# A macaron layer on one core: two fp32 tiles first, another preparation table, layers finished at their last sum, a router in four steps

## The reference

```
x = x + 0.5 * ffn(norm(x));  x = x + attention(norm(x));  x = x + 0.5 * ffn(norm(x))
attention: 16 heads of 64, causal softmax(q k^T / 8) v, then W_out
ffn: gate = u Wg^T + bias; the 4 largest of 8 are chosen, weights = softmax over them
     out = swiglu(u; Ws) + sum over 8 experts of weight_e * swiglu(u; W_e)
     swiglu(u) = (sigmoid(h) * h * v) W3^T, h = u W1^T, v = u W2^T, 341 hidden units each
```

## Time and profile before

| | |
|---|---|
| median of 3 runs | 723.57 us (723.36 to 726.57) |
| profiled execution | 728.75 us, span 727.0 us |
| mean granted TensorE clock | 0.982 |
| busy: TensorE, VectorE, ScalarE, GpSimd | 670.0, 624.5, 577.7, 482.1 us |
| DMA | mean 83 GB/s |

### The profile page before, as it was taken

The page is one execution under the profiler, slowest core; times in us unless marked ns, Lnnn a source line. Parts: engine busy times, 40 slices in busy tenths (PEclk is TensorE's granted clock), DMA queues, the critical chain, the costliest instruction groups (busy, mean ns, idle before and its releaser), DMA issues.

```text
span 727.0 us, 20474 instructions
## 1 busy us (share of the span) xinstructions
PE 670.0 (92%) x7604; PEld 444.7 (61%) x7604; DVE 624.5 (86%) x1717; ACT 577.7 (79%) x1119; POOL 482.1 (66%) x564
## 2 busy tenths in 40 slices
PE   2968997999899999899999999999999998999997
PEld 2545665555567666557656666766666766666665
DVE  2688788899999898999898999889799878889886
ACT  5887975699699889799989899988699994565553
POOL 3234655467788857788866788875488985455554
PEclk9989998999999999999999999999899999999999
DMA  7700000067598635698736689664578783000000
GB/s 205 231 1 1 2 1 1 1 95 125 96 130 138 108 59 91 116 140 131 125 59 98 100 139 144 120 88 74 74 125 140 146 128 49 15 3 1 15 2 16
DMA packets 216967, 60.58 MB, mean 83 GB/s; under 512 B 203682, under 2 KB 216100, under 8 KB 216868
## 3 DMA queue, kind: packets, MB, share of 16 engines
q1 hardware_dynamic: 216868, 59.28, 47.7%
HBM read 7.87 MB, written 1.05 MB: 12 GB/s over the span
## 4 chain that ended last, share of the span: by engine, by line
PE 41%; DVE 22%; ACT 16%; issue 11%; DMA 5%; POOL 3%; SPq 0%; ACTq 0%; DVEq 0%; POOLq 0%
PE bank L880 13%; PE bank L881 12%; PE bank L882 12%; DVE probs L1407 5%; DMA pT<-paired 5%; ACT probs L1150 4%; DVE glu L1331 4%; DVE xs L1350 3%; DVE glu L1336 3%; ACT gluh L1133 2%; PE bank L1004 2%; ACT glu L1126 2%; POOL paired L853 2%; ACT xn L1086 2%; ACT paired L1158 1%
## 5 line engine op out<-in xcount | busy, mean ns | idle before, releaser
L849 POOL TENSOR_TENSOR glul<-glu,gluh 128x512 f16<-128x512 f32 x192 | 222.5, 1161 | 136.7 <-ACT gluh L1133 134.8
L853 POOL TENSOR_TENSOR paired<-probs,paired 128x512 f16<-128x512 f32 x160 | 185.9, 1162 | 35.6 <-ACT paired L1158 34.7
L880 PE MATMUL bank<-w3h,gluh 128*128 128x128 f16 x960 | 173.3, 221 | 2.4 <-DVE w1l L1186 1.0
L1126 ACT ACTIVATE glu<-bank,tanh_scale 128x512 f32<-128x512 f32 x168 | 114.2, 680 | 74.9 <-PE bank L882 73.9
L881 PE MATMUL bank<-w3l,gluh 128*128 128x128 f16 x960 | 173.2, 221 | 0.0
L882 PE MATMUL bank<-w3h,glul 128*128 128x128 f16 x960 | 173.1, 221 | 0.0
L1331 DVE SCALAR_TENSOR_TENSOR glu<-glu,bank 128x512 f32<-128x512 f32 x168 | 114.5, 681 | 33.7 <-ACT glu L1126 32.6
L1150 ACT ACTIVATE probs<-probs,exp_bias 128x128 f32<-128x128 f32 (+3 forms) x256 | 131.6, 550 | 2.2 <-POOL exp_bias L861 2.1
L1407 DVE CUSTOM_DVE_ANT_0 probs<-bank,causal,score_scale 128x128 f32<-128x128 f32 (+3 forms) x256 | 127.9, 546 | 3.5 <-POOL paired L853 3.1
L1133 ACT ACTIVATE gluh<-glu 128x512 f16<-128x512 f32 x192 | 119.3, 622 | 6.5 <-DVE glu L1336 6.2
L1336 DVE SCALAR_TENSOR_TENSOR glu<-glu,bank 128x512 f32<-128x512 f32 x168 | 115.4, 687 | 5.8
(11 more groups left out here) (203 smaller groups left out, 1511.4 us busy)
## 6 DMA issues: line engine op xcount, KB each, us to landing
pT<-paired SPq DMA_TRANSPOSE x160, 3.3
attention_raw<-in_L_attn_W_qkv SPq DMA_DIRECT2D x6, 256.0 KB, 5.3
xs<-in_L_attn_inputs SPq DMA_DIRECT2D x4, 256.0 KB, 4.9
out<-xs SPq DMA_DIRECT2D x4, 256.0 KB, 2.3
vh<-in_L_ffn_W SPq DMA_DIRECT2D x6, 128.0 KB
pT<-in_L_ffn_W SPq DMA_DIRECT2D x6, 128.0 KB
raw_more<-in_L_ffn_W SPq DMA_DIRECT2D x4, 128.0 KB
attention_raw<-in_L_attn_W_out SPq DMA_DIRECT2D x2, 256.0 KB, 6.3
```

The source lines that it names most:

```text
L849: pool.tensor_tensor(glul[pair][:, :], g[:, :], gluh[pair][:, :], ALU.subtract).then_inc(glu_low)
L853: pool.tensor_tensor(paired[n % PAIRED][:, 1, :], probs[n % PROBS][:, :], paired[n % PAIRED][:, 0, :], ALU.subtract).then_inc(probs_low)
L880: pe.matmul(ps, high, mhigh, start=first, stop=False)
L1126: act.activation(g[:, :], psum[b1.bank][:, :], ACT.Tanh, scale=tanh_scale[:, j:j + 1]).then_inc(tanh_made)
```

## The change

Tiles 0 and 1 of layer 0 are computed natively in fp32 (`native_hidden`, `NATIVE = 2`): their weights are the turned, unscaled ones, copied by ScalarE (`copy_weights`, stage `c`), and their product is multiplied only when group 0's scales are known (`multiply_native`, VectorE). Layer 0's first norm has its fp32 copy made first. `PREPARE` and `ADDED_BY` have other values; the attention weights' measures start at step 12, not 7. Layer 0's router starts at tile 0. A feed-forward layer is in `finished` when its last `collect` is written into the list. The first attention norm has two feed-forward steps, not one, behind its statistics. The router is `gate`, `rank`, `choose`, `route`; the last holds the two products, now on GpSimd. In layer 7 tile 23 goes by halves of 256 columns through all engines (`last_hidden`), the `split_hidden` of tiles 21 and 22 come one step earlier, the collect at its step behind it, and the last rows are stored in two DMAs.

```diff
-ADDED_BY = "AAVAVAVAV"
+ADDED_BY = "VVAAAVAVV"
-PREPARE = {-3: "t0 u0 m0", -2: "m1", -1: "t1 g0 v0 s0 p0", 0: "q0 m2", 1: "r0 t3 p1 u1 q1 m3", 3: "v1 g1 r1",
-           4: "t2 s1 u2 v2 p2 q2 u3", 5: "r2 m5", 6: "m4 p3", 7: "v3 q3", 8: "g2", 9: "s2",
-           10: "t4 p4 u4 v4 q4 m6 r3", 11: "m7 r4", 12: "m8 t5 p5 u5 q5", 13: "v5 r5 g3", 14: "s3",
-           15: "u6 t6 u7 t7 p6 v6", 16: "q6 q7", 17: "p7", 18: "t8 v7", 19: "r7 r6 u8 q8", 20: "p8", 21: "v8",
-           22: "r8"}
-ROUTE_STEP = 6
+NATIVE = 2
+PREPARE = {-3: "t0 u0", -2: "c0 m0 m1", -1: "v0", 1: "u1 g0 t1 m2", 2: "s0 p0 q0 t3 p1 q1 m3 v1 g1", 3: "r0",
+           4: "t2 s1 u2 v2 p2 q2 v3", 5: "r1 r2 u3 m5", 6: "q3 p3", 7: "m4", 8: "g2 r3", 9: "s2",
+           10: "t4 p4 u4 v4 q4 m6 t5", 11: "m7 r4", 12: "v6 m8 p5 u5 q5", 13: "v5 g3", 14: "s3 r5 u7",
+           15: "u6 t6 q6 p6", 16: "q7", 17: "t7 p7", 18: "v7 r6", 19: "u8 q8", 20: "t8 p8", 21: "r7 v8 r8"}
+ROUTE_STEP = 0
+FIRST_NORM = [2, 1, 1]
-ATTENTION_MEASURES = 7
+ATTENTION_MEASURES = 12
...
+        if g == 0:
+            while self.unscaled:
+                k, glu_at, b1, b2 = self.unscaled.pop(0)
+                self.add("multiply_native", k=k, g=glu_at, b1=b1, b2=b2)
+                self.release(b2)
...
-        self.add("route", c=c)
+        self.add("rank", c=c)
+        yield
+        self.add("choose", c=c)
+        yield
+        self.add("route", c=c, left=self.route_left[c % 2])
...
+        def collect(i):
+            while collects and collects[0][0] < i:
...
+                if n == NE - 1:
+                    self.finished.add(("ff1" if c < B else "ff2", b))
...
-                if next(ending, "over") == "over" and c > 0:
-                    self.finished.add(layers[c - 1])
+                next(ending, None)
...
-            for _ in ahead:
-                yield 1.0
+            for n, _ in enumerate(ahead):
+                for _ in range(FIRST_NORM[n] if b == 0 else 1):
+                    yield 1.0
...
+                elif kind == "route":
+                    c, left = s["c"], s["left"]
+                    of = route[c % 2][:, 1:NE, :]
+                    q.wait_ge(chosen_made, c + 1)
+                    if left:
+                        q.wait_ge(drained[left.bank], left.n + left.d)
+                    done = pool.tensor_tensor(of.rearrange("p n t -> p t n"), chosen[:, :, :], over(inv_total), ALU.mult)
+                    if c:
+                        q.wait_ge(units_scaled, len(GROUPS))
+                        done.then_inc(shares_made)
+                        q.wait_ge(shares_made, c)
+                        done = pool.tensor_tensor(of, of, unscale[:, 1:NE].unsqueeze(2).broadcast_to([P, E, NT]),
+                                                  ALU.mult)
+                    done.then_inc(route_made)
...
+                elif kind == "native_hidden":
+                    for w, use in zip(native_w, (s["b1"], s["b2"])):
+                        bank_free(use)
+                        pe.matmul(psum[use.bank][:, :], w[:, cols], xnT32[:, :], start=True, stop=True
+                                  ).then_inc(filled[use.bank])
...
+                elif kind == "last_hidden":
+                    for h, (b1, b2) in enumerate(s["banks"]):
+                        part = slice(h * L // 2, (h + 1) * L // 2)
+                        for use, wh, wl in ((b1, w1h, w1l), (b2, w2h, w2l)):
+                            bank_free(use)
+                            three_pass(psum[use.bank][:, 0:L // 2], wh[:, cols], wl[:, cols], xh[:, part], xl[:, part]
+                                       ).then_inc(filled[use.bank])
...
+                        for t in range(0, NT, 2):
+                            q.wait_ge(rows_made, t // 2 + 1)
+                            sp.dma_start(chunk_of(out, b)[:, t:t + 2, :], xs[:, b * NT + t:b * NT + t + 2, :]
+                                         ).then_inc(stored, 16)
```

More of the change, by code:

```diff
@@ L196, in spread, with copy_weights @@
         self.add("scale_units", g=g)
+        if g == 0:
[3 more added lines that the diff above has]
+                self.release(b2)
+            self.scales_known = True
+    def copy_weights(self):
+        self.native_ready = [self.turned[0][k]._replace(d=1) for k in range(2)]
+        self.add("copy_weights", uses=[self.turned[0][k] for k in range(2)])
     def turn_weights(self, n, k):
-        use = self.hold_filled()
+        use = self.hold_filled(2 if n == 0 and k < 2 else 1)
         turned = self.turned.setdefault(n, {})
@@ L238, in layer_norm @@
         self.xn_left = s.use
-        self.halves_ready[halves] = s.use._replace(d=1)
-        if halves < 2:
+        self.halves_ready[halves] = s.use if i == 0 else s.use._replace(d=1)
+        if i == 0:
+            self.release(s.use)
+        elif halves < 2:
             yield
@@ L273, in hidden, with last_hidden, native_hidden @@
                  x_ready=self.halves_ready[halves], w_ready=[u for n in OWNERS[j] for u in (self.weights_ready[n, 0], self.weights_ready[n, 1])])
+        tiles[j] = {"k": k, "g": g, "b2": b2, "pair": k % GLU_PAIRS}
+    def last_hidden(self, c, j, halves, tiles):
+        k = self.tiles
+        self.tiles += 1
+        g = self.glu_taken % GLUS
+        banks = [(self.bank(), self.bank()) for _ in range(2)]
+        self.add("last_hidden", k=k, c=c, j=j, banks=banks, g=g, halves=halves, x_ready=self.halves_ready[halves],
+                 pair=k % GLU_PAIRS, left=self.pair_left[k % GLU_PAIRS])
+        tiles[j] = {"k": k, "g": g, "b2": banks[1][1], "pair": k % GLU_PAIRS}
+    def native_hidden(self, j, tiles):
+        k = self.tiles
+        self.tiles += 1
+        b1, b2 = self.bank(), self.hold_filled()
+        g = self.glu_taken % GLUS
+        self.glu_taken += 1
+        self.add("native_hidden", k=k, j=j, b1=b1, b2=b2, g=g, x_ready=self.halves_ready[0]._replace(d=1),
+                 w_ready=self.native_ready)
+        self.unscaled.append((k, g, b1, b2))
         tiles[j] = {"k": k, "g": g, "b2": b2, "pair": k % GLU_PAIRS}
@@ L301, in feed_forward @@
                 self.prepare(i)
[L302 to L310 removed]
+            at_end = c == 2 * B - 1 and i >= HT - 1
+            if not at_end:
+                collect(i)
+            if i < HT:
+                if c == 0 and i < NATIVE:
+                    assert not self.scales_known
+                    self.native_hidden(i, tiles)
+                elif not at_end:
+                    self.hidden(c, i, halves, tiles)
+                    last_b2 = tiles[i]["b2"]
+            if c == 2 * B - 1 and HT - 2 <= i < HT + SPLIT_LAG:
+                for j in {HT - 2: [HT - 4, HT - 3], HT - 1: [HT - 2]}.get(i, []):
+                    self.split_hidden(j, tiles)
+            elif SPLIT_LAG <= i < HT + SPLIT_LAG:
+                assert self.scales_known
                 self.split_hidden(i - SPLIT_LAG, tiles)
+            if at_end:
+                if i == HT - 1:
+                    self.last_hidden(c, i, halves, tiles)
+                collect(i)
             done = []
@@ L324, in feed_forward @@
             yield i >= HT - 1
-            if i == HT - 1:
+            if i == HT - 1 and not at_end:
                 self.halves_left[halves] = last_b2
@@ L635, in macaron @@
         pT = [pT_all[:, i] for i in range(TURNED)]
+        native_w = [probs[k][:, 0:NATIVE * P] for k in range(2)]
         neg_max = sb("neg_max", [P, 2, NT, 2])
```

121 lines of the change are left out of this document (94 added, 27 removed).

## The result

The changed kernel takes 705.96 us (median of 6 runs, 704.50 to 708.72); the kernel before, on the same chip, 726.32 (6 runs). The ratio is 0.9716, 95% interval 0.9693 to 0.9739: 20.4 us less. The forecast was 711.7, which was 11.9 less. The time lies in the range of 703 to 722 and the direction was right, but the size was too small by nearly half: the time is outside the 707 to 716 of the forecast's own case and nearest to the rival that it all comes through, 707.7.

A forecast was written before the change was run, and what follows sets the result against it. TensorE, busy 670.0 of 727.0 us, was taken as the bound, so gains had to be its idle or lower-clock time. Terms -0.7 + 6.5 - 0.5 + 5.5 + 4.5 + 0.6 - 4 = 11.9 us off 723.57 gave 711.7, range 703 to 722.

The forecast's parts named there:

- the forecast's own case: Whole kernel: the summed terms hold, 711.7 us, own range 707 to 716, chance 0.42.
- the rival that it all comes through: Whole kernel: no gain is given back, 707.7 us, chance 0.15.
- given back: Middle, 150 to 600 us: TensorE partly meets removed waits again in the next place, a quarter of the gains, -4 us.
- Start, -0.7: Layer 0's first tiles: fp32 products and scales make the third tile's hidden matmul later, 0.7 us lost, range -1.7 to +0.5.
- my slow case: Start: first fp32 tile at the slow rate, 4.2 us, second 2.4; third tile at 25.0, a loss of 1.5.
- ScalarE's queue in layer 0: At 36 to 50 us: attention-weight measures and table loads leave the front of tile work, +6.5 us, range 3 to 8.2.
- The rest of the table, -0.5: Layer 0's preparation: experts' measures change engines, expert 7's joining VectorE near the last maxima; 0.5 us lost, range -2.5 to +2.
- First attention norm, +5.5: End of layer 0: earlier finish and two tiles behind the statistics remove TensorE's wait and lower clock, range 0 to 6.7.
- Router, +4.5: Layer ends: two products leave VectorE for GpSimd, so a tile's multiply is not delayed, range 0 to 5.9 us.
- The rival of GpSimd's queue: Six layers: GpSimd stops for VectorE's reciprocal with low halves behind it; slower, 730.3 us, chance 0.10.
- My flag: Router: the forecast is wrong if GpSimd waits for the reciprocal over 1 us a time.
- End, +0.6: Last layer: low halves in halves and a smaller last store shorten the end by 0.6 us, range 0.2 to 1.1.

The follow-up runs named there:

- a_tbl: Kernel after with the old preparation table and engine choice, no fp32 tiles, router from tile 6, first norm split as before: 715.80 us, ratio 0.9827.
- b_fin: Kernel before with only the early finish and the first attention norm's extra step added: 724.37 us, ratio 0.9971.
- a_late: Kernel after with the early finish and the first attention norm's extra step both taken back: 702.93 us, ratio 0.9650.
- best1: a_late with the advance work of each feed-forward layer begun at step 8, not 14: 709.99 us, ratio 0.9762.
- best2: a_late with layer 4's advance work for layer 5 done at every tile step, not every second: 709.18 us, ratio 0.9754.
- b_pool: Kernel before with only the router changed, to four steps with its two products on GpSimd: 718.70 us, ratio 0.9887.
- a_end: Kernel after with its last layer as before (tile whole, old split order, one last store): 706.33 us, ratio 0.9720.
- b_m12: Kernel before with only the attention weights' sums moved from tile 7 to tile 12 of layer 0: 722.07 us, ratio 0.9938.
- b_tbl: Kernel before with fp32 tiles, new preparation table and engine choice, early router in four steps, products on VectorE: 718.44 us, ratio 0.9892.

## Why the prediction was right or wrong

The edits, each made in the kernel before and each taken back in the one after (us gained by the edit; forecast beside it). The four steps are in the second and the third number of the middle column, and in none of the last:

```
                                        forecast   alone in before   taken back in after
sums at tile 12                          } 5.3          4.5                 5.9
table, fp32 tiles, early router          }              7.8                 8.1
products on GpSimd, four steps             4.5          8.2                 6.8
early finish, first norm's step            5.5          2.1                -4.8
end                                        0.6           -                  0.3
given back                                -4.0
sum                                       11.9         22.6                16.3
```

The change measured 20.4, between the two sums. The sums are uncertain by 5 us and more, so beside the cost of the finish a give-back of a few us is neither shown nor excluded. That the time fell into the range is in part luck: the term for the norm was far too large, those for the table and the router too small, and the errors offset each other.

*Start, -0.7: the sign was wrong, inside the range.* The third tile's first f16 matmul begins at 23.05 us, 0.49 earlier than in the earlier trace rows. The two fp32 products of a tile, which no row of before could show:

```profile
10.79 3.02 PE L1054 MATMUL bank<-xnT,probs 128*128 128x512 f32 x4
...
15.19 1.92 PE L1054 MATMUL bank<-xnT,probs 128*128 128x512 f32 x4
```

That is 1.5 us a product at first and 0.96 later, where I had scaled transposes to 2.1 and 1.2. The two tiles hold TensorE for 2.86 us (10.79 to 13.65) and 1.85 (15.19 to 17.04), against 4.2 and 2.4 in my slow case: 1.9 us, the whole way from its 25.0 to 23.05. The estimate from four passes of the Trainium skill ("FP8 and Floating Point Precision", TensorE Precision Notes) was 1.5 a product, from the recorded 0.38 us of an f16 pass; the second product measured below it. Such passes follow each other every 0.21 us here, and four of these would be 0.85.

*ScalarE's queue in layer 0: the mechanism right, the size near.* I gave 6.5 to the sums and the router's table loads together. The sums alone are 4.5 to 5.9, and no wait over 2 us and no 0.50 clock stands between 40 and 60, as the test asked.

*The rest of the table, -0.5: the step that failed most.* The whole of table, fp32 tiles and router measured near 8. I had priced which engine takes which sum, and read the router's move only as table loads on ScalarE. What it also takes out, with the router in four steps, is the choice from the chain of a group's scales on VectorE, where small instructions last as long as GpSimd's (a_tbl, 1.10 and 1.18 us). Which of the three edits brings the rest stays open.

*First attention norm, +5.5: right place, size wrong, and the price of its cure missed.* The tests held: the statistics start at 101.83, 2.6 us behind the end of the ninth expert's sums (99.28), and TensorE doesn't wait for this xn. But alone the edit only brings the wait from 3.82 to 2.21 us (b_fin) and 2.1 us in all, and on top of the others there was less to take: with the router's products on GpSimd the wait is 1.9 us without this edit (a_late, best1, best2). In b_pool, where it is 1.45, it has moved rather than gone. I booked all 6.7 us of wait and lower clock on one edit and never asked what the others do at the same place. And "nothing else gets shorter by the earlier end" should have asked what gets longer: the later attention blocks stand a tile earlier, and waits for transposed probabilities go with that, for 4.8 us. A cost as large as the give-back of 4 that I spread over all terms belongs to this edit alone.

*Router, +4.5: mechanism right, sized too small.* It measured 6.8 and 8.2, each uncertain by 3. Some 6 of the 8.2 stand at its own waits; some of the rest is lower clock that went at the first norm (b_pool). The reciprocal (175.11) is followed at once by a multiply (175.21), and of the waits at tiles 48 and 72 (the test's layers 3 and 4) the first went from 2.31 to 0.93 and the second from 2.71 to 1.37, both by less than the 1.7 of the test. I had held that the choice and the comparison "go on paying" for the port pair, by the Trainium skill's rule ("SBUF — State Buffer", SBUF: two separate sides) that one engine's instruction holds it whole. The rule agrees with the rows shown: the choice, a small instruction with two inputs in SBUF, ends with the GpSimd instruction that runs at its start (1.00 to 1.10 us), and takes 0.19 where none runs. What I applied wrongly was the order: GpSimd now waits for the reciprocal and so can't hold the pair during the choice.

*The rival of GpSimd's queue* falls as a net loss, but its mechanism is real at one place, the 2.75 us wait at the end of layer 0 in b_pool. My flag, waits for the reciprocal over 1 us a time, was raised (view of waits, after):

```profile
POOL route L937 <- DVE inv_total L1464: 10.7, 6, 2.3
```

1.8 us a time, and the edit still gains 6.8. The flag took idle time of an engine that is busy 69% of the span for a cost.

*The other flag*, new waits over 2 us with a lower clock between 130 and 600, was raised too, at 227 and 571. By a_late and the pattern named there they go with the early finish, and cost less than was gained elsewhere.

*End, +0.6: right.* TensorE's last product starts at 700.36 and lasts 0.22; from its end to the end of the span it is 3.51 us, where 3.5 was the test and 3.95 the kernel before (its last: 722.85). By the times alone (a_end, 0.3 us) it can't be told from nothing.

## What to carry to other kernels

When several edits aim near one wait, ask of each what it would leave of the wait by itself; they share one gain, and each keeps its own price (here a shift of the attention blocks, 4.8 us). When a wait gets shorter, look whether what it waits for comes sooner or the waiting engine later. Price a small VectorE instruction in a critical chain by what GpSimd runs at that instant, not by its median; making GpSimd wait for the chain's result can be the cheap cure, where nothing urgent stands behind it in GpSimd's queue. Test each edit alone in the old kernel and taken back in the new one: keep the two edits mirrors of each other (here the four steps were not); the pair tells size and interaction, and here led to a kernel 0.7% faster than the change itself.

## What the runs showed of the hardware

- The same wait draws different stretches of the lower clock. Behind the first norm's wait of 3.80 to 3.82 us came 6.8 us at 0.50 in the kernel before, and 3.4 in b_m12 and b_tbl; behind the wait of 2.31 us 3.4 in the kernel before and none in b_tbl. One trace is one execution: on one chip the kernel before ran at mean granted clocks of 0.983 to 0.992, with spans of 726.2 to 728.2 us at the lower end and 721.4 at the upper. So what a wait costs beside itself is known only afterwards. The four stretches of the kernel before cost 10.7 us, the three of the kernel after 5.8: about 5 of the 22.9 us between the two traces.
- ScalarE's sum of magnitudes is two instructions, 0.62 and 0.19 us, one every 0.81 us where they follow each other.
- A [128x10] `TENSOR_SCALAR` with one input was held up by GpSimd like a two-input one: 1.18 us in a_tbl and 0.90 in the kernel before, for 0.17 in b_pool and 0.33 in b_m12.
